# A recurrence of 3136 steps on one core: one chain of 32 images, or two chains of 16 in turn with longer filler matmuls

## The chip, the cores and the metric

The kernel runs on one core of a Trainium2 chip. The metric is the device time of one execution in microseconds (us), the median of several runs. The core has five engines: TensorE (PE; its weight loads are listed apart as PEld), VectorE (DVE), ScalarE (ACT), GpSimd (POOL) and SyncE (SP), which here issues all the DMAs. The profile tells of one more thing that matters here, the clock granted to TensorE: 1.00 in its rows is 2.4 GHz, and the lower level, 1.2 GHz, is half of that.

## What is computed

The program is two layers of a network on 32 images of 56 x 56 pixels with 128 channels. Layer 0 is windowed attention and a mixture of experts, layer 1 a focal convolution and, last, a recurrence over the 3136 pixels of each image. Only the recurrence is touched by the change. Cut to what matters:

```python
x = x + _L0_conv_ref(_ln_c(x), ...)          # attention in windows of 7 x 7
t = t + _L0_ffn_ref(_ln_t(t), ...)           # mixture of 8 experts
x = x + _L1_conv_ref(_ln_c(x), ...)          # focal convolution
t = t + _L1_ffn_ref(_ln_t(t), ...)           # the recurrence, below

def _L1_ffn_ref(x, W, V, gamma, beta):       # x: 32 images, 3136 tokens, 128 channels
    Wx = jnp.einsum('bti,hi->bth', x, W)
    mean, var = jnp.mean(flat, axis=0), jnp.var(flat, axis=0)      # flat: all tokens of Wx
    Wx = ((flat - mean) * jax.lax.rsqrt(var + BN_EPS) * gamma + beta).reshape(B, T, H)
    def step(yt, wx_t):
        yt = jax.nn.sigmoid(wx_t + yt @ V.T)
        return (yt, yt)
    _, ys = jax.lax.scan(step, y0, jnp.swapaxes(Wx, 0, 1))
    return jnp.swapaxes(ys, 0, 1)
```

Step t needs the result of step t - 1, so the 3136 steps are a chain. The 32 images are independent of one another.

## The kernel before

Six stages run one after the other; each has its own program on each engine, written out by hand, and semaphores between them. The stage that matters is `recurrent_stage`, the last one. The other five are the same before and after. Their names in the trace begin with `att`, `moe`, `foc`, `conv` and `mod`; those of the recurrence begin with `rec`.

The recurrent stage works in chunks of `TC` = 16 steps, 196 of them. The channels lie on the partitions, the images in the columns. For each chunk the tokens are loaded, normalized (DVE statistics, POOL scaling into `xn`), turned by TensorE into `pin` (four transposes, `turn_in`, L2407), copied by DVE into `xT`, and multiplied by the weights into the PSUM tile `ph` (`drive`, L2417: four pieces of 128 columns, each as four matmuls that write 32 partitions). After that `ph` holds wx_t for the 16 steps. Then each step of the chain is two links:

- TensorE adds V times the result of the step before onto 32 columns of `ph` (`add`, L2435: four fp32 matmuls, each with 32 columns of weights and 32 output partitions; the trace lists each as two records, so x8 for an add). It waits for the semaphore `moved`, and raises `added`.
- ScalarE takes the sigmoid of these 32 columns into `yT` (L2314). It waits for `added`, and raises `moved`.

The finished chunk is turned back by four transposes (`turn_out`, L2425, into `pout`), and DVE adds the residual (`finish`) and SP stores it. TensorE does the work of the neighbouring chunks between the adds: step 0 to 3 of a chunk hold one `turn_in` transpose each, steps 4 to 7 one `turn_out` each, steps 12 to 15 one piece of `drive` each. Behind the transposes, and in steps 8 to 11 alone, stands filler: four bf16 matmuls of 256 columns (384 in steps 8 to 11) into `p_idle` (L2466), whose result nobody reads. The order of TensorE's program is that of the Python text in `step`, and TensorE works through it in this order.

A matmul that takes 32 columns of weights fills a quarter of the array's columns; the trace writes it as 128*32 (rows * columns of the array). A transpose here is 128*128. Four matmuls of the form 128*32 that write different quarters of the partitions run beside one another. The words "tiling" and "form of the array" below mean this pair of numbers.

TensorE's loop is written out for two chunks (`U // 2`), and taken around some 97 times.

Of the kernel before, what the change touches and what calls it, by code (L numbers as in the profile page):

```python
# [19 lines left out]
ACT = mybir.ActivationFunctionType  # L20
AX = mybir.AxisListType

P = 128
C = 128
# [9 lines left out]
BANK = 512  # L34
# [60 lines left out]
def hold(eng, sem, value, ticks):  # L95


    eng.wait_ge(sem, value)
    eng.sem_inc(ticks, 1)
# [2067 lines left out]
def recurrent_stage(nc, B, x3, gram, W, w_t, v_t, gamma, beta, ident, out):  # L2167
# [6 lines left out]
    TC = 16  # L2174
    N = PIX // TC
    COLS_ = TC * B
    SUB = 4
    TT = TC // SUB
    ROWS = TT * B
# [3 lines left out]
    S = Stage(nc, "rec")  # L2183
    with S.ctx:
# [4 lines left out]
        vt = S.sb("vt", [C, C])  # L2189
# [4 lines left out]
        wbn = S.sb("wbn", [C, C])  # L2194
# [15 lines left out]
        idle_x = S.ctx.enter_context(nc.sbuf_tensor("rec_idle_x", [C, 384], mybir.dt.bfloat16))  # L2210
        p_idle = S.ps("p_idle", [P, BANK])

        pin = S.ps("pin", [P, BANK])
        pout = S.ps("pout", [P, BANK])
        ph = S.ps("ph", [P, 2, BANK])
        ps = S.ps("ps", [P, BANK])

        ticks = S.sem("ticks")
# [3 lines left out]
        stats_part, stats, eps_added, rstd_done, normed = (S.sem(k) for k in ("stats_part", "stats", "eps_added", "rstd_done", "normed"))  # L2222
        turned, xT_out = S.sem("turned"), S.sem("xT_out")
        driven = S.sem("driven")
        added, moved = S.sem("added"), S.sem("moved")
        y_turned, res_made = S.sem("y_turned"), S.sem("res_made")
        stored = S.sems("stored", 2)
        block = S.block()
        CONSTS = 16 * 7

        def column(t):

            at = (t % SUB) * ROWS + (t // SUB) * B
            return slice(at, at + B)

        @block.sync
        def _(sp):
# [65 lines left out]
        @block.scalar  # L2303
        def _(act):

            def step(n, first, last):
                a = n.slot(2)
                for t in range(TC):
                    cs = column(t)
                    if t == 0 and first >= 2:  # L2310
                        act.wait_ge(y_turned, n.val(1, -1))
                        act.sem_inc(ticks, 1)
                    act.wait_ge(added, n.val(TC, t + 1))
                    act.activation(yT[:, a, cs], ph[:, a, cs], ACT.Sigmoid).then_inc(moved, 1)  # L2314

            run_steps(act, N, U, step)

# [73 lines left out]
        def _(pe):  # L2391
# [19 lines left out]
            def drive(n, piece):  # L2411

                if piece == 0:
                    pe.wait_ge(xT_out, n.val(1, 1))
                cs = slice(piece * ROWS, (piece + 1) * ROWS)
                for r in range(0, C, 32):
                    ins = pe.matmul(ph[r:r + 32, n.slot(2), cs], wbn[:, r:r + 32], xT[:, n.slot(2), cs],  # L2417
                                    start=(piece == 0), stop=False, skip_group_check=True)
                if piece == SUB - 1:
                    ins.then_inc(driven, 1)  # L2420

# [6 lines left out]

            pe.wait_ge(setup, 13)

            def add(n, cs, before):


                for r in range(0, C, 32):
                    ins = pe.matmul(ph[r:r + 32, n.slot(2), cs], vt[:, r:r + 32], before, start=False, stop=True,  # L2435
                                    skip_group_check=True)
                ins.then_inc(added, 1)

            def step(n, first, last):
                a = n.slot(2)  # L2440
                if first == 0:
                    for sub in range(SUB):
                        turn_in(n, sub)
                    for piece in range(SUB):
                        drive(n, piece)
                for t in range(TC):
                    cs = column(t)
                    if t == 0 and first == 0:

                        add(n, cs, y0[:])  # L2450
                    else:
                        before = yT[:, a, column(t - 1)] if t else yT[:, 1 - a, column(TC - 1)]
                        pe.wait_ge(moved, n.val(TC, t))
                        add(n, cs, before)

                    if t < SUB and last < -1:
                        turn_in(n + 1, t)
                    if SUB <= t < 2 * SUB and first >= 1:
                        turn_out(n - 1, t - SUB, first - 1)
                    if t >= 3 * SUB:  # L2460
                        if last < -1:
                            drive(n + 1, t - 3 * SUB)
                        continue

                    for r in range(0, C, 32):
                        pe.matmul(p_idle[r:r + 32, 0:384 if t >= 2 * SUB else 256], idle_w[:, r:r + 32],  # L2466
                                  idle_x[:, 0:384 if t >= 2 * SUB else 256], start=True, stop=True)
                if last == -1:
                    pe.wait_ge(moved, n.val(TC, TC))
# [100 lines left out]
```

## Time and profile before

| what | value |
|---|---|
| median of 3 runs | 8683.52 us (8679.89 to 8687.49) |
| profiled execution, from its first to its last instruction | 8678.4 us |
| recurrent stage in it, from the first add to the last sigmoid | some 1838 us, from 6833 to 8671 us |
| TensorE busy over the span | 90% |
| granted clock in the middle of the recurrent stage | 1.00 |

The profile is of one execution. Its span is 5.1 us below the median of the runs, which is what lies around the span and between executions. Busy TensorE time is no measure here, since the modelled ends of matmuls overlap and since filler counts as work. How to read it: a step of the chain is found in the list of instructions in order of time, as the distance from one add to the next, and what stands between them tells which engine the chain waits for.

### The profile page before, as it was taken

The numbers are of one execution on the slowest core, as the hardware profiler recorded it, in microseconds if no ns is written. First come the engines' busy times: TensorE is split into PE (matmuls) and PEld (weight loads), VectorE is DVE, ScalarE is ACT, GpSimd is POOL, SyncE is SP. The second block draws the span as 40 slices with busy tenths as digits, with TensorE's granted clock in tenths as the row PEclk, the third lists the DMA queues.
The fourth block names the chain that finished last, engine by engine and source line by source line (L and its number), as shares of the span: only waits on it lengthen the run. The fifth ranks groups of instructions, "written<-read, shape, count | busy, mean of one in ns | idle before, by whom it ended". The sixth has DMA issues, their size and how long they took to land. (4 is left out here: it accounts for less than half of the span.)

```text
span 8678.4 us, 336810 instructions
## 1 busy us (share of the span) xinstructions
PE 7853.7 (90%) x120363; PEld 5180.1 (60%) x120363; DVE 6360.4 (73%) x21127; ACT 4495.5 (52%) x12517; POOL 5624.9 (65%) x6959
## 2 busy tenths in 40 slices
PE   7999999979999999869989999997999788888888
PEld 6777777754444444447767766655777555555554
DVE  7999999979999999878857777777888422222222
ACT  5666666645655555559933333335666333333333
POOL 8888888868888888768812222225777544444444
PEclk9999999989999999989999999999999899999999
DMA  1222222211111111148855555538888222222221
GB/s 52 58 58 58 58 58 58 57 55 58 57 56 56 56 59 57 63 157 300 295 189 187 180 188 190 193 132 219 232 231 229 77 56 57 56 56 56 56 57 53
DMA packets 797829, 958.44 MB, mean 110 GB/s; under 512 B 323100, under 2 KB 661825, under 8 KB 773584
## 3 DMA queue, kind: packets, MB, share of 16 engines
q1 hardware_dynamic: 797264, 952.06, 35.9%
q8 instruction: 214, 3.51, 0.2%
q14 instruction: 351, 2.88, 0.1%
HBM read 574.81 MB, written 453.35 MB: 118 GB/s over the span
## 5 line engine op out<-in xcount | busy, mean ns | idle before, releaser
L991 PE MATMUL moe_pe_out<-moe_we,moe_xnT 128*128 128x512 f32 x3136 | 1482.0, 607 | 179.2 <-DVE moe_acc L885 172.3
L1595 PE MATMUL conv_pc<-conv_c,conv_toep 64*64 64x432 f32 (+1 forms) x12260 | 1356.3, 527 | 2.5 <-ACT conv_c L1497 2.5
L2314 ACT ACTIVATE rec_yT<-rec_ph 128x32 f32<-128x32 f32 x3136 | 618.3, 197 | 1242.5 <-PE rec_ph L2435 1242.5
L787 ACT ACTIVATE moe_scaled<-moe_pe_out,moe_gate 128x128 f32<-128x128 f32 x3136 | 892.0, 367 | 692.6 <-PE moe_pe_out L991 690.6
L991 PEld LDWEIGHTS moe_pe_out<-moe_we,moe_xnT 128*128 128x128 f32 x3136 | 546.8, 191 | 942.4 <-issue 940.9
L1452 POOL TENSOR_TENSOR conv_g<-conv_c,conv_gate 128x896 f32<-128x896 f32 x128 | 366.6, 2864 | 1123.8 <-DVE conv_out L1565 1086.2
L2361 DVE COPY rec_xT<-rec_pin 128x512 f32<-128x512 f32 x196 | 135.6, 692 | 1240.1 <-PE rec_pin L2407 1240.1
L1595 PEld LDWEIGHTS conv_pc<-conv_c,conv_toep 64*64 64x64 f32 (+1 forms) x12260 | 855.3, 133 | 310.9 <-issue 108.8
L2435 PE MATMUL rec_ph<-rec_yT,rec_vt 128*32 128x32 f32 x25080 | 844.5, 207 | 195.5 <-ACT rec_yT L2314 120.8
L307 POOL TENSOR_SCALAR att_xn<-att_xin,att_mv,att_rstd 128x128 f32<-128x128 f32 x1024 | 881.9, 871 | 54.1 <-POOL att_rstd L303 54.1
L2435 PEld LDWEIGHTS rec_ph<-rec_yT,rec_vt 128*32 128x32 f32 x25080 | 496.9, 108 | 646.9 <-ACT rec_yT L2314 608.9
L2466 PE MATMUL rec_p_idle<-rec_idle_x,rec_idle_w 128*32 128x256 bf16 (+1 forms) x9408 | 718.5, 299 | 0.0
L725 POOL TENSOR_TENSOR moe_paired<-moe_scaled 128x256 f32<-128x256 f32 x784 | 582.6, 743 | 171.2 <-ACT moe_scaled L787 150.6
L2289 POOL TENSOR_SCALAR rec_xn<-rec_xin,rec_mv,rec_rstd 128x127 f32<-128x127 f32 x784 | 634.0, 821 | 41.5 <-POOL rec_rstd L2286 41.5
L2284 POOL TENSOR_SCALAR rec_rstd<-rec_mv 128x4 f32<-128x4 f32 x196 | 45.6, 233 | 893.0 <-DVE rec_mv L2356 863.7
L1595 PE MATMUL conv_pc<-conv_cin,conv_toep 64*64 64x448 f32 (+1 forms) x3048 | 522.1, 536 | 56.6 <-DMA conv_toep<-rows_dram 33.9
L1470 ACT ACTIVATE conv_c<-conv_pc,conv_gap 128x448 f32<-128x448 f32 x256 | 148.2, 630 | 689.7 <-PE conv_pc L1595 689.7
L718 POOL TENSOR_SCALAR moe_xn<-moe_xin,moe_mv,moe_rstd 128x127 f32<-128x127 f32 x560 | 483.8, 864 | 0.4 <-POOL moe_rstd L712 0.4
L1932 ACT ACTIVATE mod_z<-mod_xin,mod_nmean,mod_rstd_x 112x128 f32<-112x128 f32 x896 | 368.9, 483 | 168.8 <-DVE mod_nmean L2038 167.2
L330 ACT ACTIVATE att_prT<-att_pb 128x512 f32<-128x512 f32 x512 | 287.6, 597 | 234.1 <-PE att_pb L519 234.1
L312 POOL TENSOR_TENSOR att_xin<-att_xin,att_bproj 128x512 f32<-128x512 f32 x256 | 389.0, 1520 | 21.4
L733 POOL TENSOR_TENSOR moe_others<-moe_paired 128x128 f32<-128x128 f32 x784 | 360.4, 460 | 51.4 <-DVE moe_acc L930 33.9
(212 smaller groups left out, 19859.0 us busy)
## 6 DMA issues: line engine op xcount, KB each, us to landing
conv_toep<-rows_dram SPq DMA_DIRECT2D x32, 2304.0 KB, 13.7
c<-foc_cs SPq DMA_DIRECT2D x32, 1792.0 KB, 10.9
conv_cin<-c SPq DMA_DIRECT2D x32, 1792.0 KB, 10.2
ctx_all<-conv_out SPq DMA_DIRECT2D x32, 1792.0 KB, 6.5
att_xin<-x_windows SPq DMA_DIRECT2D x512, 98.0 KB
moe_xin<-x SPq DMA_DIRECT2D x112, 448.0 KB, 3.5
x<-moe_acc SPq DMA_DIRECT2D x112, 448.0 KB, 2.7
foc_xin<-x SPq DMA_DIRECT2D x32, 1568.0 KB, 8.3
```

The lines of the kernel that those rows point to most:

```text
L307: ins = pool.tensor_scalar(xn[:, a, t, :], xin[:, s, t, :], mv[:, a, t, 0:1], rstd[:, a, t:t + 1], ALU.subtract, ALU.mult)
L312: pool.tensor_tensor(xin[:, s, :, :], xin[:, s, :, :], bproj[:].unsqueeze(1).to_broadcast([P, PAIRS, C]), ALU.add).then_inc(bproj_added, 1)
L718: pool.tensor_scalar(xn[:, a, t, 0:C - 1], xin[:, n.slot(4), t, 0:C - 1], mv[:, a, t, 0:1], rstd[:, a, t:t + 1], ALU.subtract, ALU.mult).t ...
L725: pool.tensor_tensor(paired[:, b, :, :], scaled[:, b, 0:2, :], scaled[:, b, 2:4, :], ALU.add)\
L787: ins = act.activation(scaled[:, b, e, :], pe_out[:, b, 1, e * C:(e + 1) * C], ACT.Identity, scale=g)
L991: pe.matmul(pe_out[:, b, half, :], xnT[:, n.slot(2), t, :], we[:, half * 4:half * 4 + 4, :].rearrange("d e c -> d (e c)"), start=True, sto ...
L1595: return pe.matmul(image_pairs(pc[k], half)[m0:m1, :, i0:i1], w, tile[r0:r1, images(half), i0 + away:i1 + away], start=start, stop=True, s ...
L1932: ins = act.activation(z[:, b, t, 0:C], xin[:, m.slot(2), GRP * c + t, :], ACT.Identity, bias=nmean[:, b, t:t + 1], scale=rstd_x[:, b, t:t ...
L2289: ins = pool.tensor_scalar(xn[:, a, t, 0:C - 1], xin[:, n.slot(4), t, 0:C - 1], mv[:, a, t, 0:1], rstd[:, a, t:t + 1], ALU.subtract, ALU.mult)
L2314: act.activation(yT[:, a, cs], ph[:, a, cs], ACT.Sigmoid).then_inc(moved, 1)
L2435: ins = pe.matmul(ph[r:r + 32, n.slot(2), cs], vt[:, r:r + 32], before, start=False, stop=True, skip_group_check=True)
L2466: pe.matmul(p_idle[r:r + 32, 0:384 if t >= 2 * SUB else 256], idle_w[:, r:r + 32], idle_x[:, 0:384 if t >= 2 * SUB else 256], start=True, ...
```

## The change

The 32 images are split into two halves of 16 (`HALF`). Each half has its own chain: its own columns of PSUM (`ph` gets one more dimension, so that each half has a bank of its own for each of the two chunks in flight), its own `added` and `moved` semaphores, its own sigmoid of 16 columns. In each step TensorE's program is now: add of half 0, something, add of half 1, filler of 512 columns. The something is the `turn_in` transpose in steps 0 to 3, the `turn_out` transpose in steps 4 to 7, filler of 256 columns in steps 8 to 11, and a piece of `drive` in steps 12 to 15. `drive` writes the two halves by matmuls of 64 columns each, twice as many as before. The filler is no longer four matmuls of 32 weight columns, but two of 64 (`idle`). The filler that stood behind the transposes is gone; the one of 512 columns stands in every step. The loop over two chunks now holds 416 matmuls of the source, where it held 272. Semaphores that were waited for once in a step are waited for once per half.

```diff
-        ph = S.ps("ph", [P, 2, BANK])
+        ph = S.ps("ph", [P, 2, 2, BANK])
...
-        added, moved = S.sem("added"), S.sem("moved")
+        added, moved = S.sems("added", 2), S.sems("moved", 2)
...
-                    act.wait_ge(added, n.val(TC, t + 1))
-                    act.activation(yT[:, a, cs], ph[:, a, cs], ACT.Sigmoid).then_inc(moved, 1)
+                    for half in range(2):
+                        act.wait_ge(added[half], n.val(TC, t + 1))
+                        act.activation(yT[:, a, column(t, half)], ph[:, a, half, sums(t)], ACT.Sigmoid).then_inc(moved[half], 1)
...
-                for r in range(0, C, 32):
-                    ins = pe.matmul(ph[r:r + 32, n.slot(2), cs], wbn[:, r:r + 32], xT[:, n.slot(2), cs],
-                                    start=(piece == 0), stop=False, skip_group_check=True)
+                out = slice(piece * TT * HALF, (piece + 1) * TT * HALF)
+                for half in range(2):
+                    x = xT[:, n.slot(2), cs].rearrange("p (t b) -> p t b", b=B)[:, :, half * HALF:(half + 1) * HALF]
+                    for r in range(0, C, 32):
+                        ins = pe.matmul(ph[r:r + 32, n.slot(2), half, out].rearrange("p (t b) -> p t b", b=HALF), wbn[:, r:r + 32], x,
+                                        start=(piece == 0), stop=False, skip_group_check=True)
...
+            def add(n, t, half, first):
+                if t == 0 and first == 0:
+                    before = y0[:, 0:HALF]
+                else:
+                    before = yT[:, n.slot(2), column(t - 1, half)] if t else yT[:, 1 - n.slot(2), column(TC - 1, half)]
+                    pe.wait_ge(moved[half], n.val(TC, t))
                 for r in range(0, C, 32):
+                    ins = pe.matmul(ph[r:r + 32, n.slot(2), half, sums(t)], vt[:, r:r + 32], before, start=False, stop=True,
                                     skip_group_check=True)
-                ins.then_inc(added, 1)
+                ins.then_inc(added[half], 1)
+
+            def idle(columns):
+                for r in range(0, C, 64):
+                    pe.matmul(p_idle[r:r + 64, 0:columns], idle_w[:, r:r + 64], idle_x[:, 0:columns], start=True, stop=True)
...
                 for t in range(TC):
+                    add(n, t, 0, first)
                     if t < SUB and last < -1:
                         turn_in(n + 1, t)
-                    if SUB <= t < 2 * SUB and first >= 1:
+                    elif SUB <= t < 2 * SUB and first >= 1:
                         turn_out(n - 1, t - SUB, first - 1)
-                    if t >= 3 * SUB:
-                        if last < -1:
-                            drive(n + 1, t - 3 * SUB)
-                        continue
-
-                    for r in range(0, C, 32):
-                        pe.matmul(p_idle[r:r + 32, 0:384 if t >= 2 * SUB else 256], idle_w[:, r:r + 32],
-                                  idle_x[:, 0:384 if t >= 2 * SUB else 256], start=True, stop=True)
+                    elif t >= 3 * SUB and last < -1:
+                        drive(n + 1, t - 3 * SUB)
+                    else:
+                        idle(256)
+                    add(n, t, 1, first)
+                    idle(512)
```

How the instructions stand in TensorE's program before, inside the loop, at step 7 of a chunk (a `turn_out`) and steps 8 and 9 (filler alone). The last number of a row is partitions x columns of the output; a REGISTER_ALU works out the value of the next wait:

```order
L2435 MATMUL rec_ph<-rec_yT,rec_vt 32x32 x4
L2425 MATMUL rec_pout<-rec_idn,rec_yT 128x128
L2466 MATMUL rec_p_idle<-rec_idle_x,rec_idle_w 32x256 x4
L2453 REGISTER_ALU
L2435 MATMUL rec_ph<-rec_yT,rec_vt 32x32 x4
L2466 MATMUL rec_p_idle<-rec_idle_x,rec_idle_w 32x384 x4
L2453 REGISTER_ALU
L2435 MATMUL rec_ph<-rec_yT,rec_vt 32x32 x4
L2466 MATMUL rec_p_idle<-rec_idle_x,rec_idle_w 32x384 x4
```

The same place of TensorE's program now:

```order
L2450 MATMUL rec_ph<-rec_yT,rec_vt 32x16 x4
L2435 MATMUL rec_pout<-rec_idn,rec_yT 128x128
L2450 MATMUL rec_ph<-rec_yT,rec_vt 32x16 x4
L2456 MATMUL rec_p_idle<-rec_idle_x,rec_idle_w 64x512 x2
L2448 REGISTER_ALU
L2450 MATMUL rec_ph<-rec_yT,rec_vt 32x16 x4
L2456 MATMUL rec_p_idle<-rec_idle_x,rec_idle_w 64x256 x2
L2450 MATMUL rec_ph<-rec_yT,rec_vt 32x16 x4
L2456 MATMUL rec_p_idle<-rec_idle_x,rec_idle_w 64x512 x2
```

Between two adds of one chain stand now the other chain's add and one filler of 512 columns in two pieces of 64 partitions, beside the transpose or the shorter filler. Four changes of the form of the array lie in each step (32 to 128 or 64, back to 32, to 64, back to 32), where step 7 had two and steps 8 and 9 none.

Steps 12 and 13 in TensorE's program before, with the pieces of `drive`:

```order
L2435 MATMUL rec_ph<-rec_yT,rec_vt 32x32 x4
L2417 MATMUL rec_ph<-rec_xT,rec_wbn 32x128 x4
L2453 REGISTER_ALU
L2435 MATMUL rec_ph<-rec_yT,rec_vt 32x32 x4
L2417 MATMUL rec_ph<-rec_xT,rec_wbn 32x128 x4
```

And now:

```order
L2450 MATMUL rec_ph<-rec_yT,rec_vt 32x16 x4
L2427 MATMUL rec_ph<-rec_xT,rec_wbn 32x64 x8
L2450 MATMUL rec_ph<-rec_yT,rec_vt 32x16 x4
L2456 MATMUL rec_p_idle<-rec_idle_x,rec_idle_w 64x512 x2
L2448 REGISTER_ALU
L2450 MATMUL rec_ph<-rec_yT,rec_vt 32x16 x4
L2427 MATMUL rec_ph<-rec_xT,rec_wbn 32x64 x8
L2450 MATMUL rec_ph<-rec_yT,rec_vt 32x16 x4
L2456 MATMUL rec_p_idle<-rec_idle_x,rec_idle_w 64x512 x2
```

The `drive` steps had no filler, and every matmul in them had the form 128*32. Now the filler of 512 columns stands in them too, with two changes of form in each.

## Rows read from the trace of the kernel before

**Rows 1.** Stretches of the recurrent stage, middle part; columns in the first line.
```profile
core 0: us, PE busy (x) PEld busy (x) DVE busy (x) ACT busy (x) POOL busy (x), PEclk, DMA share, GB/s
7450.00:8050.00 600.00, 535.99 (x13860) 306.48 (x13856) 162.85 (x640) 202.27 (x1026) 289.04 (x387) 1.00 0.21 56
```

**Rows 2.** Who waited for whom from 6850 to 8650 us: total, times, longest.
```profile
ACT rec_yT L2314 <- PE rec_ph L2435: 1193.8, 3078, 0.8
```

**Rows 3.** Order of time, a filler step: start, duration (us), engine, instruction, [idle before].
```profile
7607.31 0.20 ACT L2314 ACTIVATE rec_yT<-rec_ph 128x32 f32<-128x32 f32 x1 [0.39 <-PE rec_ph L2435]
...
7607.56 0.27 PE L2435 MATMUL rec_ph<-rec_yT,rec_vt 128*32 128x32 f32 x8 [0.15 <-ACT rec_yT L2314]
...
7607.65 0.35 PE L2466 MATMUL rec_p_idle<-rec_idle_x,rec_idle_w 128*32 128x384 bf16 x4
...
7607.90 0.20 ACT L2314 ACTIVATE rec_yT<-rec_ph 128x32 f32<-128x32 f32 x1 [0.39 <-PE rec_ph L2435]
7608.15 0.16 PEld L2435 LDWEIGHTS rec_ph<-rec_yT,rec_vt 128*32 128x32 f32 x8 [0.41 <-ACT rec_yT L2314]
```

**Rows 4.** The same view, a step with a `turn_in` transpose.
```profile
7602.31 0.27 PE L2435 MATMUL rec_ph<-rec_yT,rec_vt 128*32 128x32 f32 x8
...
7602.51 0.33 PE L2407 MATMUL rec_pin<-rec_idn,rec_xn 128*128 128x128 f32 x1
...
7602.76 0.29 PE L2466 MATMUL rec_p_idle<-rec_idle_x,rec_idle_w 128*32 128x256 bf16 x4
...
7602.89 0.27 PE L2435 MATMUL rec_ph<-rec_yT,rec_vt 128*32 128x32 f32 x8
```

**Rows 5.** The same view, TensorE alone, a step with a piece of `drive`.
```profile
7600.55 0.27 PE L2435 MATMUL rec_ph<-rec_yT,rec_vt 128*32 128x32 f32 x8
7600.64 0.40 PE L2417 MATMUL rec_ph<-rec_xT,rec_wbn 128*32 128x128 f32 x8
```

**Rows 6.** The same view, TensorE alone, in the attention stage, two places.
```profile
600.94 0.60 PE L474 MATMUL att_pf<-att_idn,att_xn 128*128 128x128 f32 x4
...
903.22 0.82 PE L483 MATMUL att_pf<-att_xnT,att_wqkv 128*128 128x392 f32 x2
903.97 0.90 PE L532 MATMUL att_pb<-att_prT,att_vv 49*32 49x49 f32 x64
904.79 0.49 PE L491 MATMUL att_pf<-att_wqkv,att_xnT 128*49 128x64 f32 x10
```

**Rows 7.** Groups by form: busy us, mean ns of one | idle before.
```profile
L2435 PE MATMUL rec_ph<-rec_yT,rec_vt 128*32 128x32 f32 x25080 | 844.5, 207 | 195.5 <-ACT rec_yT L2314 120.8
L2466 PE MATMUL rec_p_idle<-rec_idle_x,rec_idle_w 128*32 128x256 bf16 x6272 | 461.1, 284 | 0.0
L2417 PE MATMUL rec_ph<-rec_xT,rec_wbn 128*32 128x128 f32 x6272 | 318.1, 275 | 0.8 <-DVE rec_xT L2361 0.8
L2466 PE MATMUL rec_p_idle<-rec_idle_x,rec_idle_w 128*32 128x384 bf16 x3136 | 273.5, 329 | 0.0
L1595 PEld LDWEIGHTS conv_pc<-conv_c,conv_toep 64*64 64x64 f32 x12248 | 853.1, 133 | 308.4 <-issue 106.4
L2435 PEld LDWEIGHTS rec_ph<-rec_yT,rec_vt 128*32 128x32 f32 x25080 | 496.9, 108 | 646.9 <-ACT rec_yT L2314 608.9
L330 ACT ACTIVATE att_prT<-att_pb 128x512 f32<-128x512 f32 x512 | 287.6, 597 | 234.1 <-PE att_pb L519 234.1
L2314 ACT ACTIVATE rec_yT<-rec_ph 128x32 f32<-128x32 f32 x3136 | 618.3, 197 | 1242.5 <-PE rec_ph L2435 1242.5
```

**Rows 8.** Code: two loops' stretches, then the DMA queues in the second.
```profile
432.92:460.75 27.83, 26.73 (x737) 21.21 (x738) 26.70 (x61) 17.43 (x33) 24.86 (x28) 1.00 0.20 54
...
4831.00:4921.00 90.00, 88.65 (x1017) 63.88 (x1013) 65.16 (x57) 34.35 (x64) 22.64 (x8) 1.00 0.55 187
...
q8 instruction: 9, 0.15, 0.8%
```

More of the change, by code:

```diff
@@ L2209, in recurrent_stage @@
         idle_w = S.ctx.enter_context(nc.sbuf_tensor("rec_idle_w", [C, C], mybir.dt.bfloat16))
-        idle_x = S.ctx.enter_context(nc.sbuf_tensor("rec_idle_x", [C, 384], mybir.dt.bfloat16))
+        idle_x = S.ctx.enter_context(nc.sbuf_tensor("rec_idle_x", [C, 512], mybir.dt.bfloat16))
         p_idle = S.ps("p_idle", [P, BANK])
@@ L2229, in recurrent_stage, with column, sums @@
         CONSTS = 16 * 7
-        def column(t):
-            at = (t % SUB) * ROWS + (t // SUB) * B
-            return slice(at, at + B)
+        HALF = B // 2
+        def column(t, half):
+            at = (t % SUB) * ROWS + (t // SUB) * B + half * HALF
+            return slice(at, at + HALF)
+        def sums(t):
+            at = (t % SUB) * TT * HALF + (t // SUB) * HALF
+            return slice(at, at + HALF)
         @block.sync
@@ L2308, in step @@
                 for t in range(TC):
-                    cs = column(t)
                     if t == 0 and first >= 2:
@@ L2429, in _ @@
             pe.wait_ge(setup, 13)
-            def add(n, cs, before):
+            def add(n, t, half, first):
[4 more added lines that the diff above has]
+                    pe.wait_ge(moved[half], n.val(TC, t))
                 for r in range(0, C, 32):
-                    ins = pe.matmul(ph[r:r + 32, n.slot(2), cs], vt[:, r:r + 32], before, start=False, stop=True,
+                    ins = pe.matmul(ph[r:r + 32, n.slot(2), half, sums(t)], vt[:, r:r + 32], before, start=False, stop=True,
                                     skip_group_check=True)
-                ins.then_inc(added, 1)
+                ins.then_inc(added[half], 1)
+            def idle(columns):
+                for r in range(0, C, 64):
+                    pe.matmul(p_idle[r:r + 64, 0:columns], idle_w[:, r:r + 64], idle_x[:, 0:columns], start=True, stop=True)
             def step(n, first, last):
-                a = n.slot(2)
                 if first == 0:
@@ L2446, in step @@
                 for t in range(TC):
[L2447 to L2454, printed above, removed]
+                    add(n, t, 0, first)
                     if t < SUB and last < -1:
                         turn_in(n + 1, t)
-                    if SUB <= t < 2 * SUB and first >= 1:
+                    elif SUB <= t < 2 * SUB and first >= 1:
                         turn_out(n - 1, t - SUB, first - 1)
-                    if t >= 3 * SUB:
-                        if last < -1:
-                            drive(n + 1, t - 3 * SUB)
-                        continue
-                    for r in range(0, C, 32):
-                        pe.matmul(p_idle[r:r + 32, 0:384 if t >= 2 * SUB else 256], idle_w[:, r:r + 32],
-                                  idle_x[:, 0:384 if t >= 2 * SUB else 256], start=True, stop=True)
+                    elif t >= 3 * SUB and last < -1:
[4 more added lines that the diff above has]
+                    idle(512)
                 if last == -1:
-                    pe.wait_ge(moved, n.val(TC, TC))
+                    for half in range(2):
+                        hold(pe, moved[half], n.val(TC, TC), ticks)
                     for sub in range(SUB):
```

## The prediction

> **What bounds the kernel now.** First the stretches of the recurrent stage [rows 1]: in 600 us there are 1026 sigmoids, one in 0.585 us; the clock is 1.00 throughout, the level of 2.4 GHz; every engine but TensorE is busy for less than half of the time. Since the stage takes 3136 steps, it takes 3136 x 0.585 = 1834 us, a fifth of the span, and every nanosecond of a step is worth 3.1 us.
>
> Then who waits for whom [rows 2]: ScalarE waited 1193.8 us for the adds in 3078 steps, 0.39 us a step; with its own 0.197 us [rows 7] this is the whole step. So the period is the round trip of one chain. The step with filler alone shows its links [rows 3]: the add begins at 7607.56, its sigmoid at 7607.90 (0.34 later), takes 0.20, and the next add begins 0.05 after its end. The add has waited: TensorE was done with the filler. In a step with a transpose there is no such wait [rows 4], yet the step is just as long, 7602.31 to 7602.89. There TensorE's own work fills the step by itself: add 0.20, transpose 0.25, filler 0.13. The reader is to see that TensorE has slack only where no transpose stands.
>
> The third thing is what a change of the array's form costs. The modelled end of a matmul is start plus duration. Where the next matmul has the same form, it begins 0.16 to 0.18 before that end: filler 7602.76 + 0.29 = 7603.05, the add at 7602.89 [rows 4]; add 7607.56 + 0.27 = 7607.83, filler at 7607.65 [rows 3]. Where the form changes, it begins only 0.07 to 0.08 before it: add (128\*32) to transpose (128\*128) 7602.58 against 7602.51, transpose to filler 7602.84 against 7602.76 [rows 4]; and with no transpose in it, 128\*128 to 49\*32 at 904.04 against 903.97, and 49\*32 to 128\*49 at 904.87 against 904.79 [rows 6]. So TensorE runs nearly empty at each change, and an add that takes 0.09 when filler of its own form follows [rows 3] takes 0.20 ahead of another form.
>
> **The change part by part.** TensorE takes its program in order, so in each step it does add, something, add, filler of 512, whichever chain is ready. I cost each piece as the time from its start to the start of the next.
>
> *Two chains.* Each chain has 16 columns. An fp32 column costs (275 - 207) / (128 - 32) = 0.7 ns [rows 7], so an add becomes 0.011 shorter, no more: the four weight loads and two records of each stay. A sigmoid shrinks by 16 x (597 - 197) / (512 - 32) = 0.013 [rows 7]. A chain's round trip becomes 0.585 - 0.024 = 0.561. That is the floor of a step, provided that TensorE's pieces sum to less; the two sigmoids, 2 x 0.184, fit into it.
>
> *Add ahead of another form:* 0.20 - 0.011, taken as 0.186 with the rounding of the rows (bounds 0.18 and 0.19). Of the same form, ahead of `drive`: 0.09 - 0.01 = 0.08.
>
> *Transposes*, unchanged: 0.256 (0.25 to 0.26) [rows 4].
>
> *Filler, two matmuls of 128\*64.* No row shows this form. The nearest is the filler of 128\*32 behind a transpose: 0.29 - 0.075 = 0.215 to a change of form [rows 4]. Weights of 64 columns take longer to load than of 32, by 133 - 108 = 25 ns in fp32 [rows 7]; here between 0 and that, and I take 0.007, since bf16 is half the bytes and part is hidden. So 0.222 for 256 columns (0.215 to 0.24). For 512 there are 256 columns more, at (329 - 284) / 128 = 0.35 ns [rows 7] 0.09, at the full 2.4 GHz 0.107: I take 0.325 (0.31 to 0.34). The two halves of the array work side by side, as the four quarters do in [rows 3].
>
> *`drive` pieces.* The same columns in twice the matmuls. Add to `drive` is 0.09 and `drive` 0.40 long, 0.17 of which overlaps the next add of the same form [rows 5]: 0.32, less 0.01 for the shorter add, 0.315 for both (0.30 to 0.33).
>
> *The form changes* decide. The rows show a change from 32 to 128, 128 to 32, and between two partial forms (49\*32 to 128\*49), all with the same result. 32 to 64 columns at 128 rows stands in no row. The Trainium skill states it in general, in TensorEngine Tiling (Array Packing), Key Properties: "Changing tiling mode (not just tile) drains the TensorE". By that rule the pair here is no exception; by the rows alone it is a close neighbour of what they show, and I cost it so and price the opposite below.
>
> *Sums.* Steps with a transpose (8 of 16): 0.186 + 0.256 + 0.186 + 0.325 = 0.953. Steps with both fillers (4): 0.186 + 0.222 + 0.186 + 0.325 = 0.919. Steps with `drive` (4): 0.315 + 0.186 + 0.325 = 0.826. The mean is (8 x 0.953 + 4 x 0.919 + 4 x 0.826) / 16 = 0.913. All three lie far above the 0.561 of a chain, so TensorE's order becomes the bound, and the latency that the second chain hides is not on the path any more. Against 0.585 that is +0.328 a step, 3136 x 0.328 = +1029 us. The span goes from 8678.4 to 9707; with the 5.1 us between span and median, 9712. I say **9710**.
>
> *At nothing:* DVE, POOL and SP have 16 x 0.9 = 14.6 us for a chunk instead of 9.4, and waited before. The second sigmoid lies beside the filler. The waits per half stand in TensorE's queue ahead of the other chain's add, but the sigmoid waited for was over some 0.35 us earlier. The first and last dozen steps run at the lower clock and may add some 10 us, within the range. If the filler were not there (its cover for nothing but the clock), the sum would be 0.6 to 0.63 in the transposing steps and the chain 0.561 elsewhere: even then not much is won.
>
> **The bounds.** All low ends together: steps of 0.92, 0.885 and 0.79, mean 0.879, +922 us, 9605. All high ends: 0.98, 0.955 and 0.86, mean 0.944, +1126 us, 9810. I widen the lower side to 9560, since the form of 64 is not shown and the next add's weights may come in a little sooner.
>
> **The rivals.**
> *The array goes from 32 to 64 columns without running empty.* For it: no row shows this pair, and the weights of 32 and 64 columns might share a setting. Against: every change that the rows do show costs the same, 49\*32 to 128\*49 included. Then an add ahead of filler takes 0.08, filler 0.225 (512) or 0.13 (256): steps of 0.186 + 0.256 + 0.08 + 0.225 = 0.747, 0.561 (the chain; TensorE's pieces sum to 0.515) and 0.315 + 0.08 + 0.225 = 0.62, mean 0.669, +262 us, **8946**. With the drain in one direction only, the mean is about 0.78 to 0.79 and the time some **9300**.
> *The chains win.* If no change of form at all cost more than columns, the longest step would be 0.08 + 0.15 (four transposes in a row end after 0.60 in all [rows 6]) + 0.08 + 0.225 = 0.535, below 0.561; the stage would run at the chain's 0.561, 0.024 x 3136 = 75 us faster, **8608**. The place is TensorE's order in the transposing steps, and the point from which it decides is a sum under 0.561. Against it speak both changes in [rows 4], which alone make 0.44 of add and transpose.
> *Code loading.* The loop now has 256 x 4 (adds) + 64 x 4 (`drive`) + 16 x 2 (transposes) + 80 x 2 (filler) = 1472 matmul and weight-load records where it had 864. The attention loop has 737 + 738 = 1475 in an iteration of 27.83 us, and no block of code is read in it; the convolution's has 1017 + 1013 in 90 us, and 9 blocks are read [rows 8]. So 1472 should stay loaded. The Trainium skill, in Runtime: NRT & Kernel Launch, Instruction fetch mechanics, gives TensorE room for 2048 instructions, but also says that a branch back beyond two pages of code must wait for a read; by the first the loop stays, by the second each turn stalls. The rows of the attention loop agree with the first. If it stalled, one read in each of 97 turns: 0.8% of 16 engines' 90 us over 9 blocks is 1.28 us each [rows 8], 124 us on top, **9836**.
> *The two halves of the filler run one after the other:* +0.21 in every step and more in four, over **10,400**. [rows 3] show four quarters at once, so this is remote.
>
> **How the numbers follow.** Forecast 0.84; 32 to 64 for free 0.05, one way 0.03; code loading 0.03; halves in turn 0.01; chains win 0.03; and 0.01 that terms cancel to about the time before. Of the forecast's 0.84 nearly all lies in 9560 to 9830, so this range holds the time about 8 times in 10 and need not reach a rival. A measurement of this kernel can tell about 0.2%, 17 us, from no change. Faster by more 0.03, within it 0.01, slower 0.96.
>
> **What would show it.** Right: ScalarE's 6272 sigmoids of about 184 ns, two in each 0.91 us; no idle time of TensorE before an add; filler of 512 beginning 0.07 before the modelled end of the add ahead of it, and an add 0.07 before the filler's end; steps of three lengths, 0.95, 0.92 and 0.83. Wrong: filler beginning 0.08 after the start of an add (first rival); adds that still wait for sigmoids in most steps (chains win); reads of code in the middle of the stage (code loading).

## The result, and the profile after

The changed kernel takes 9737.3 us (9733.2 to 9737.8), the kernel before 8685.5 in the runs beside it: 1.121 times as long, 95% interval 1.1195 to 1.1223. The forecast was 9710, with a range from 9560 to 9830. The profiled execution of the changed kernel spans 9735.2 us, 1056.8 more than before. Some executions of several kernels here take some 40 us longer, and in the one of them that was traced (the run in two quarters, below) the attention stage, which the change does not touch, ended at 1876.0 us instead of 1832 to 1838, so differences are also read from the recurrent stage alone, from the start of its first sigmoid to that of its last: 1838.0 us before, 2891.7 us now.

The stretch in the middle of the recurrent stage, in the view of [rows 1]:

```profile
core 0: us, PE busy (x) PEld busy (x) DVE busy (x) ACT busy (x) POOL busy (x), PEclk, DMA share, GB/s
7450.00:8050.00 600.00, 600.00 (x15031) 361.15 (x15029) 104.07 (x410) 240.43 (x1306) 185.12 (x246) 1.00 0.14 36
```

There are 1306 sigmoids, each of half the images, so 653 steps in 600 us: 0.919 us a step where [rows 1] gave 0.585. The clock is 1.00 as before, so TensorE is not slower; it has more to do in each step. It is busy without a gap, 600.00 of 600. Who waited for whom from 6850 to 9700 us, to set against [rows 2] (total, times, longest):

```profile
ACT rec_yT L2321 <- PE rec_ph L2450: 1605.2, 5373, 0.6
PEld rec_ph L2450 <- issue: 705.4, 3098, 0.4
...
PEld rec_ph L2450 <- ACT rec_yT L2321: 0.2, 1, 0.2
```

ScalarE still waits for adds, but no add waits for a sigmoid any more, except one. TensorE's own order sets the step. In order of time (start, duration, engine, instruction), first a step with a transpose, then one with both fillers, then one with a piece of `drive`:

```profile
7994.47 0.26 PE L2450 MATMUL rec_ph<-rec_yT,rec_vt 128*32 128x16 f32 x8
7994.65 0.33 PE L2435 MATMUL rec_pout<-rec_idn,rec_yT 128*128 128x128 f32 x1
7994.91 0.26 PE L2450 MATMUL rec_ph<-rec_yT,rec_vt 128*32 128x16 f32 x8
7995.10 0.41 PE L2456 MATMUL rec_p_idle<-rec_idle_x,rec_idle_w 128*64 128x512 bf16 x2
7995.44 0.26 PE L2450 MATMUL rec_ph<-rec_yT,rec_vt 128*32 128x16 f32 x8
...
8000.21 0.26 PE L2450 MATMUL rec_ph<-rec_yT,rec_vt 128*32 128x16 f32 x8
8000.40 0.30 PE L2456 MATMUL rec_p_idle<-rec_idle_x,rec_idle_w 128*64 128x256 bf16 x2
8000.62 0.26 PE L2450 MATMUL rec_ph<-rec_yT,rec_vt 128*32 128x16 f32 x8
8000.81 0.41 PE L2456 MATMUL rec_p_idle<-rec_idle_x,rec_idle_w 128*64 128x512 bf16 x2
8001.15 0.26 PE L2450 MATMUL rec_ph<-rec_yT,rec_vt 128*32 128x16 f32 x8
...
7988.18 0.26 PE L2450 MATMUL rec_ph<-rec_yT,rec_vt 128*32 128x16 f32 x8
7988.26 0.41 PE L2427 MATMUL rec_ph<-rec_xT,rec_wbn 128*32 128x64 f32 x16
7988.49 0.23 PE L2450 MATMUL rec_ph<-rec_yT,rec_vt 128*32 128x16 f32 x8
7988.65 0.41 PE L2456 MATMUL rec_p_idle<-rec_idle_x,rec_idle_w 128*64 128x512 bf16 x2
7988.99 0.26 PE L2450 MATMUL rec_ph<-rec_yT,rec_vt 128*32 128x16 f32 x8
```

The steps are 0.97, 0.94 and 0.81 us long. At every change of form the next matmul begins 0.07 to 0.08 before the modelled end of the one ahead, here also between 32 and 64 columns: 8000.21 + 0.26 = 8000.47 against 8000.40, 8000.81 + 0.41 = 8001.22 against 8001.15. Where the form stays (add to `drive`, 7988.44 against 7988.26) it is 0.18. This is the pair that no row of before showed, and it behaves as the others.

### The profile page after: what moved, and what is told of

The parts are those of the page before. It is cut to its first block and busy times, and to the rows that moved or that the text cites. A ratio compares the mean times of both kernels' runs of the same rounds, so it can differ in the third digit from the quotient of the medians.

```text
span 9735.2 us, 399581 instructions
## 1 busy us (share of the span) xinstructions
PE 9107.2 (94%) x150179; PEld 6007.5 (62%) x150179; DVE 6362.9 (65%) x21127; ACT 5035.8 (52%) x15653; POOL 5631.5 (58%) x6959
## 5 line engine op out<-in xcount | busy, mean ns | idle before, releaser
L2321 ACT ACTIVATE rec_yT<-rec_ph 128x16 f32<-128x16 f32 x6272 | 1155.2, 184 | 1759.2 <-PE rec_ph L2450 1654.5
L2450 PEld LDWEIGHTS rec_ph<-rec_yT,rec_vt 128*32 128x32 f32 x50160 | 1010.3, 108 | 1001.3 <-issue 717.9
L2450 PE MATMUL rec_ph<-rec_yT,rec_vt 128*32 128x16 f32 x50160 | 1583.0, 192 | 0.0
L2456 PE MATMUL rec_p_idle<-rec_idle_x,rec_idle_w 128*64 128x512 bf16 (+1 forms) x7864 | 1518.3, 383 | 0.0
L1595 PEld LDWEIGHTS conv_pc<-conv_c,conv_toep 64*64 64x64 f32 (+1 forms) x12260 | 877.1, 133 | 282.0 <-issue 95.3
L2456 PEld LDWEIGHTS rec_p_idle<-rec_idle_x,rec_idle_w 128*64 128x64 bf16 x7864 | 430.9, 106 | 108.9
```

The lines of the kernel that those rows point to most:

```text
L1595: return pe.matmul(image_pairs(pc[k], half)[m0:m1, :, i0:i1], w, tile[r0:r1, images(half), i0 + away:i1 + away], start=start, stop=True, s ...
L2321: act.activation(yT[:, a, column(t, half)], ph[:, a, half, sums(t)], ACT.Sigmoid).then_inc(moved[half], 1)
L2450: ins = pe.matmul(ph[r:r + 32, n.slot(2), half, sums(t)], vt[:, r:r + 32], before, start=False, stop=True, skip_group_check=True)
L2456: pe.matmul(p_idle[r:r + 64, 0:columns], idle_w[:, r:r + 64], idle_x[:, 0:columns], start=True, stop=True)
```

## The experiments

Theory: the change of form between adds (32 columns) and filler (64) makes TensorE run empty twice more in each step, and with that its pieces sum to more than the round trip of a chain. Rivals: the columns of filler cost, in whatever form; the step is held by another link; code is loaded.

**Filler of the adds' form, in four quarters.**

```diff
-                for r in range(0, C, 64):
-                    pe.matmul(p_idle[r:r + 64, 0:columns], idle_w[:, r:r + 64], ...)
+                for r in range(0, C, 32):
+                    pe.matmul(p_idle[r:r + 32, 0:columns], idle_w[:, r:r + 32], ...)
```

> The changed kernel with its filler of 256 and 512 columns in four matmuls of 32 weight columns (the form of the adds) where it has two of 64; columns and places stay. Theory (a change of the array's form lets TensorE run empty, and this sets the step): the add ahead of the filler shrinks from 0.19 to 0.08 us and the filler from 0.33 to 0.22; steps of 0.75 us with a transpose, 0.56 (one chain's round trip) with both fillers, 0.59 with a piece of drive, mean 0.66; time 8,935 us. Rival (the columns of filler cost, whatever their form): steps and time stay, 9,737 us.

Measured 9613 us (9595 to 9630): the theory's time missed by far, and yet not for the rival's reason. Where no code was read, the steps were as short as the theory gives or shorter (0.56 to 0.58 with filler or `drive`, 0.72 with a transpose), but every second turn of TensorE's loop (32 steps) took some 34 us instead of 20.9. At such a turn, in order of time, TensorE alone:

```profile
8161.90 0.40 PE L2456 MATMUL rec_p_idle<-rec_idle_x,rec_idle_w 128*32 128x512 bf16 x4
8166.98 0.31 PE L2450 MATMUL rec_ph<-rec_yT,rec_vt 128*32 128x16 f32 x8 [4.68 <-issue]
8167.22 0.48 PE L2414 MATMUL rec_pin<-rec_idn,rec_xn 128*128 128x128 f32 x1
```

TensorE stands still for 4.68 us with no semaphore to wait for (in the kept trace it is the branch at the loop's end that takes 4.9 us on average at such turns, and 0.2 at the others), and the transpose after it takes 0.48 instead of 0.33: the clock has fallen (granted 0.84 on average from 7450 to 8050 us). The DMA queues from 7000 to 8600 us show why, ahead of those of the changed kernel from 7000 to 9600:

```profile
q8 instruction: 252, 4.13, 1.2%
...
q1 hardware_dynamic: 67889, 92.76, 13.6%
q14 instruction: 19, 0.16, 0.0%
```

252 blocks of code are read here through q8, nine in each of the long turns and none in the short ones, and none in the changed kernel. The queue q14, with a read now and then in both, goes with no standstill. The filler's four matmuls instead of two make 1632 records in the loop where the changed kernel has 1472, and it does not stay loaded. So this run mixed two causes, and the next two runs take them apart.

**Two quarters: the adds' form, the loop as long as in the changed kernel.**

```diff
-                for r in range(0, C, 64):
-                    pe.matmul(p_idle[r:r + 64, 0:columns], idle_w[:, r:r + 64], ...)
+                for r in range(0, 64, 32):
+                    pe.matmul(p_idle[r:r + 32, 0:columns], idle_w[:, r:r + 32], ...)
```

> The changed kernel with each filler as two matmuls of 32 weight columns, so that the filler has the adds' form and the loop as many matmuls as in the changed kernel (a quarter of the array's columns each, half of it unused). It repeats the run with four quarters without its longer code. Theory (change of form): transposing steps 0.72 us, all others 0.56, mean 0.64, no code read in the middle of the stage, 8,850 us. Rival (the columns cost, and the four quarters gained little because columns are what counts): above 9,600 us.

Measured 8891 us (8869 to 8913), no code read. A step with a transpose, in order of time, TensorE alone:

```profile
7908.60 0.26 PE L2450 MATMUL rec_ph<-rec_yT,rec_vt 128*32 128x16 f32 x8
7908.68 0.38 PE L2456 MATMUL rec_p_idle<-rec_idle_x,rec_idle_w 128*32 128x512 bf16 x2
7908.74 0.37 PE L2450 MATMUL rec_ph<-rec_yT,rec_vt 128*32 128x16 f32 x8
7909.05 0.33 PE L2435 MATMUL rec_pout<-rec_idn,rec_yT 128*128 128x128 f32 x1
7909.30 0.26 PE L2450 MATMUL rec_ph<-rec_yT,rec_vt 128*32 128x16 f32 x8
```

The filler begins 0.08 after the add (0.19 in the changed kernel). Of the next add's eight records, four begin 0.06 after the filler and four some 0.16 later, which fits the two quarters that the filler leaves free. The step is 0.70, the others 0.56 to 0.58. With columns, places and number of matmuls as in the changed kernel, 870 of the 1054 us by which the recurrent stage had grown are gone (it takes 2022.0 us; by the medians, 846 of 1052). The forecast was 8850. This filler covers only half of the array, so the free half could have had a part in the gain. But the run with four quarters covers all of it, and its undisturbed turns take 20.9 us against 20.5 here and 29.4 in the changed kernel. The form was the cost. What stays above the kernel before is the transposing steps, whose own two changes of form no filler touches, and some 0.3 us where the loop turns back.

**The same form, twice the matmuls of half the columns.**

```diff
+                for part in range(2):
+                    cs = slice(part * columns // 2, (part + 1) * columns // 2)
                     for r in range(0, C, 64):
-                        pe.matmul(p_idle[r:r + 64, 0:columns], ...)
+                        pe.matmul(p_idle[r:r + 64, cs], ...)
```

> The changed kernel with each filler cut into twice as many matmuls of half the columns, the form of 64 columns kept: the loop gets as many records as in the run with four quarters (1632 against 1472), and nothing else changes. Theory (the longer loop does not stay loaded): blocks of code are read throughout the stage and a turn waits for them, 9,950 to 10,400 us. Rival (what the run with four quarters lost was due to its filler or its clock, not to code): 9,740 us, no code read.

Measured 10,518 us, more than the upper end. The stretch from 7450 to 8050 us, and TensorE's code queue from 7000 to 8600:

```profile
7450.00:8050.00 600.00, 545.14 (x12895) 332.74 (x12893) 79.01 (x310) 185.85 (x1010) 140.87 (x188) 0.80 0.12 31
...
q8 instruction: 275, 4.51, 1.3%
```

The steps that are not disturbed keep their length (0.97, 0.94, 0.81), but there are 505 steps in 600 us instead of 653: code is read, and the clock is at 0.80 on average. So code loading is real, 160 records above the changed kernel. It costs some 780 us, where the prediction gave 124 for one read a turn. In 63 of 95 turns nine blocks are read, and such a turn takes 41.9 us instead of 29.5. Some 4.4 us of this is the standstill at the branch. The rest lies in the steps behind it: most of the next chunk's take 1.3 to 1.45 us at the lower clock.

**One chain, filler in halves.** In the kernel before only the filler's form is changed, as `C, 32` to `C, 64` and `r + 32` to `r + 64`.

> The kernel before (one chain of 32 images) with its filler of 256 and 384 columns in two matmuls of 64 weight columns where it has four of 32. Theory: the eight steps with a transpose become 0.20 + 0.26 + 0.22 = 0.68 us, since the filler is now drained before the next add; the steps with filler alone stay at 0.585, because add and filler take 0.47 there and the chain is waited for anyway; mean 0.63, time 8,833 us. Rival (the two halves are harmless, and only the doubled adds and the longer filler cost): 8,685 us. Second rival (the two halves run one after the other): transposing steps of 0.79 and filler steps of 0.63, 9,050 us.

Measured 8876 us (8855 to 8898, two runs), slower than the kernel before by 1.1 to 3.0%. The recurrent stage takes 2008.2 us, 170 more than before, where the theory gives 148. A step with a transpose, TensorE alone, then two steps with filler alone:

```profile
7905.42 0.27 PE L2435 MATMUL rec_ph<-rec_yT,rec_vt 128*32 128x32 f32 x8
7905.62 0.33 PE L2407 MATMUL rec_pin<-rec_idn,rec_xn 128*128 128x128 f32 x1
7905.88 0.30 PE L2466 MATMUL rec_p_idle<-rec_idle_x,rec_idle_w 128*64 128x256 bf16 x2
...
7900.51 0.27 PE L2435 MATMUL rec_ph<-rec_yT,rec_vt 128*32 128x32 f32 x8
7900.71 0.35 PE L2466 MATMUL rec_p_idle<-rec_idle_x,rec_idle_w 128*64 128x384 bf16 x2
7901.10 0.27 PE L2435 MATMUL rec_ph<-rec_yT,rec_vt 128*32 128x32 f32 x8
```

The transposing step grows from 0.585 to 0.69, the others stay at 0.585 although their filler now begins 0.20 after the add instead of 0.09 [rows 3]. A change of form costs nothing where the chain is waited for anyway, and its whole price where TensorE has no slack. The halves run side by side: a transposing step would be 0.79 if they did not.

**256 columns instead of 512 behind the second half.** One word: `idle(512)` becomes `idle(256)`.

> The changed kernel with 256 columns instead of 512 in the filler behind the second half, all else as it is. Theory (TensorE's order is the bound in every step): each step loses 256 columns at 2.4 GHz, 0.107 us; 3136 x 0.107 = 335 us, 9,402 us. Rival (another link, a chain's round trip or ScalarE, holds the step): less than 100 us, above 9,640 us.

Measured 9429 us (9413 to 9445); the recurrent stage takes 2566.7 us, 325 less than in the changed kernel, where 335 were forecast. The stretch from 7450 to 8050 us:

```profile
7450.00:8050.00 600.00, 600.00 (x17013) 408.50 (x17014) 117.12 (x460) 272.13 (x1477) 207.74 (x276) 1.00 0.15 41
```

1477 sigmoids are 738.5 steps, 0.812 us each, 0.106 less than in the changed kernel, nearly all of the forecast 0.107. So nothing but TensorE's order holds the step.

**Any change of form.** The filler becomes one matmul of 128 weight columns over the whole array:

```diff
-                for r in range(0, C, 64):
-                    pe.matmul(p_idle[r:r + 64, 0:columns], idle_w[:, r:r + 64], ...)
+                pe.matmul(p_idle[:, 0:columns], idle_w[:], idle_x[:, 0:columns], start=True, stop=True)
```

> The changed kernel with each filler as one matmul of 128 weight columns, same columns and places. Theory (any change of form makes TensorE run empty, whichever two forms they are): the same steps as in the changed kernel, give or take the longer load of the weights, 9,740 to 9,850 us. Rival (only the pair of 32 and 64 is dear): 9,400 us or less.

Measured 9680 us, 0.6% below the changed kernel, so the range was missed on the low side and the rival is out. A filler behind an add of the second half:

```profile
7908.12 0.39 PE L2455 MATMUL rec_p_idle<-rec_idle_x,rec_idle_w 128*128 128x512 bf16 x1
7908.44 0.25 PE L2450 MATMUL rec_ph<-rec_yT,rec_vt 128*32 128x16 f32 x8
```

Again the next matmul begins 0.07 before the end. The filler takes 0.32 where two halves take 0.34, though its weights are twice as wide. The loads of the filler's weights (least, median and longest time in ns, behind the colon), in the kernel before, the changed kernel and this run:

```profile
L2466 PEld LDWEIGHTS rec_p_idle<-rec_idle_x,rec_idle_w x9408: 91/93/133, 6833.9 to 8667.9; 128*32 128x32 bf16 x196
...
L2456 PEld LDWEIGHTS rec_p_idle<-rec_idle_x,rec_idle_w x7864: 106/106/128, 6836.6 to 9726.8; 128*64 128x64 bf16 x197
...
L2455 PEld LDWEIGHTS rec_p_idle<-rec_idle_x,rec_idle_w x3932: 95/95/103, 6840.0 to 9670.0; 128*128 128x128 bf16 x197
```

So 128 columns load in 95 ns where 64 take 106, which is some 0.011 of the 0.02. The Trainium skill says in TensorE: Matmul & The Clock Gate, Weight-path perf modes, that bf16 weights of full width load faster; the trace agrees, 95 ns against 106.

**No filler at all.** `idle(256)` and `idle(512)` are left out; `p_idle` stays unwritten.

> The changed kernel without any filler (p_idle is not written; no result depends on it). Theory: TensorE's pieces sum to 0.53 us in the transposing steps and less elsewhere, so each step is one chain's round trip, 0.561 us at a granted clock of 1.00: about 8,615 us, a little faster than the kernel before. If the clock falls to 1.2 GHz without filler: adds of 0.26, transposes of 0.31 and a chain of 0.63, mean step 0.65, about 8,890 us. Rival (two chains in turn have a cost of their own besides form and filler): well above both.

Measured 8733 us (8716 to 8772), between the two cases named, 0.4% slower than the kernel before:

```profile
7450.00:8050.00 600.00, 544.95 (x20424) 419.39 (x20428) 158.06 (x621) 297.13 (x1994) 282.05 (x375) 0.85 0.20 55
```

Steps at the full clock are 0.558 long, the round trip of a chain of 16 images that the prediction had at 0.561; but the granted clock is 0.85 on average, and 997 steps in 600 us are 0.602 each. With the new order of VectorE (below) and still no filler:

> The run without filler, with VectorE's statistics of chunk n + 2 ahead of the copy of chunk n + 1. Theory (at the chunk's end the first transpose waits for the normalized chunk, and this loop of TensorE, VectorE and POOL holds the chunk at 9.6 us): that wait goes, the boundary steps fall from 0.8 to 1.2 us to 0.56 to 0.65, and the time to 8,640 to 8,690 us; the clock stays below 1.00 in places. Rival (the clock alone makes those steps long): 8,730 us as without the new order.

Measured 8721 us (8698 to 8778), not the 8640 to 8690 of the theory. The medians are not clearly apart, but the recurrent stage is 34 us shorter in the traces (1855.5 us against 1889.6): three transposes wait for normalizing instead of 40, and the granted clock is 0.91 instead of 0.85 in the middle. Why the clock is higher is not shown. The steps where the loop turns back are as long as before (0.92 to 1.19 us). I had put them down to normalizing; that was wrong, as the next run shows.

**Two chains where they fit.** Filler of the adds' form only where TensorE has room, and VectorE's statistics earlier:

```diff
                 for t in range(TC):
                     add(n, t, 0, first)
...
+                    elif 2 * SUB <= t < 3 * SUB:
+                        idle(384, 4)
                     add(n, t, 1, first)
-                    idle(512)
+                    if 2 * SUB <= t < 3 * SUB:
+                        idle(384, 4)
+                    elif t >= 3 * SUB:
+                        idle(256, 2)
...
-                if last < -1:
-                    drive(n + 1)
                 if last < -2:
                     ...
                     layer_stats(n + 2)
+                if last < -1:
+                    drive(n + 1)
```

Here `idle(columns, parts)` writes `parts` quarters, each with 32 weight columns.

> Two chains with filler of the adds' form alone, and only where TensorE has room: 384 columns in four quarters behind each half in steps 8 to 11, 256 in two quarters behind the second half in steps 12 to 15, none beside the transposes; 1472 records in the loop as in the changed kernel. Besides, VectorE takes the statistics of chunk n + 2 before the copy of chunk n + 1, so that normalizing does not wait for the transposes. Theory: TensorE's pieces stay below a chain's round trip of 0.559 us in all steps, and the statistics come early enough: 8,605 us, 0.9% faster than the kernel before, at a granted clock near 1.00. Rival (without filler beside the transposes the clock falls): 8,650 to 8,730 us.

Measured 8677 us, 0.998 of the kernel before (0.9965 to 0.9994): faster, but by far less than the forecast (9 us in the recurrent stage, 1828.7 us, where 83 were forecast). From the run before it differs by the filler alone, and the stage is 27 us shorter, so here the filler pays for itself. The clock is 1.00, and 29 of the loop's 32 steps take 0.56 to 0.57. Two places cost more, together some 60 us. Where the loop turns back, once in 32 steps, 0.41 us is lost (order of time, TensorE and ScalarE):

```profile
7715.29 0.28 PE L2456 MATMUL rec_p_idle<-rec_idle_x,rec_idle_w 128*32 128x256 bf16 x2
7715.53 0.18 ACT L2321 ACTIVATE rec_yT<-rec_ph 128x16 f32<-128x16 f32 x1 [0.15 <-PE rec_ph L2450]
7715.70 0.26 PEld L2450 LDWEIGHTS rec_ph<-rec_yT,rec_vt 128*32 128x32 f32 x8 [0.34 <-ACT rec_yT L2321]
```

The sigmoid that this add needs was over at 7715.38; the add should have begun at 7715.43 and began at 7715.70. The branch lies between: in the kept trace it takes from 7715.35 to 7715.56. The view puts the wait down to a sigmoid, but that is not it. The rest of the 0.41 lies mostly in the add itself, whose sigmoid begins 0.39 after it, instead of 0.32 elsewhere. And in step 8 of each chunk 0.11 us is lost, where the distance between the two chains changes from that of the transposing steps (0.45) to that of the filler steps; the next run bears this out, since it keeps the distance and the loss is gone.

**The pair first, then the work.** In the same kernel both adds stand at the head of the step and the work behind them: transposes in steps 0 to 7, `drive` and `idle(256, 2)` in 8 to 11, twice `idle(384, 4)` in 12 to 14, nothing in 15.

> The last candidate (two chains, filler of the adds' form, VectorE's statistics ahead of its copy) with another order in TensorE's step: both adds at once, and the work behind them; transposes in steps 0 to 7, drive and 256 columns of filler in two quarters in steps 8 to 11, 768 columns in four quarters in steps 12 to 14, nothing in step 15, where the loop turns back. Theory (that candidate loses 0.41 us where the loop turns back, once in 32 steps, since TensorE has only a short gap between adds there, and 0.11 us in step 8, where the distance between the two chains has to change): both go, every step is a round trip of 0.559 us, 8,620 us, 0.8% faster than the kernel before. Rival (the two sigmoids stand so close that ScalarE delays the second chain, or the branch costs as before): 8,660 us or above.

Measured 8632 us, 0.9946 of the kernel before (0.993 to 0.9963), the fastest of all. The view of [rows 1], and two steps at 7909 us:

```profile
7450.00:8050.00 600.00, 583.43 (x24033) 407.11 (x24025) 167.76 (x669) 299.48 (x2136) 300.62 (x400) 1.00 0.22 59
...
7909.24 0.36 PE L2450 MATMUL rec_ph<-rec_yT,rec_vt 128*32 128x16 f32 x16
7909.56 0.28 ACT L2321 ACTIVATE rec_yT<-rec_ph 128x16 f32<-128x16 f32 x2 [0.27 <-PE rec_ph L2450]
7909.80 0.36 PE L2450 MATMUL rec_ph<-rec_yT,rec_vt 128*32 128x16 f32 x16
```

1068 steps in 600 us, 0.562 each; the recurrent stage takes 1781.6 us, 56 less than before. Where the loop turns back a step takes 0.57 to 0.74, on average 0.65, not 0.97. The two sigmoids lie side by side in 0.28 us.

**The same with VectorE's old order.** The last piece of the diff above is undone.

> The same kernel with VectorE's order as it was (copy first, then the statistics). Theory (the loop of transposes, copy, statistics and normalizing takes some 9.2 us, more than 16 steps of 0.559, 8.94 us): the first transpose of a chunk waits some 0.2 us, 16 to 40 us slower than with the new order. Rival (the loop fits into a chunk): the same time within 0.2%.

Measured 8655 us (0.9951 to 0.9977 of the kernel before), 23 us above the new order. What the transposes of `turn_in` waited for over the whole span, first here, then with the new order (total, times):

```profile
POOL rec_xn L2296: 44.9, 188
...
POOL rec_xn L2296: 8.5, 3
```

In 188 of 196 chunks the first transpose waits for the normalized chunk, 0.24 us a time. The step there takes 0.69 in one of the loop's two chunks, and 0.56 or 0.68 in the other, instead of 0.56. So this loop does not fit into 16 steps of 0.559, though it fits into 16 of 0.585. Not all of the difference is this wait: in eight turns of the loop the clock fell for a while and some 2 us were lost each time, with the new order in three, so some 10 of the 27 us by which the stage is longer (1809.1 us) belong to the clock.

## Why the prediction was right

**The bound before** was read rightly: a round trip of one chain. The run with one chain and filler in halves grew by 0.10 in the steps without slack and by nothing in the others (but for those at the loop's turn).

**The change of form** was the one step without a row of its own. It was costed by its neighbours, and the trace after bears it out: 0.07 before the end at each change between 32 and 64. The run in two quarters shows what that is worth: 870 us of the 1054 in the recurrent stage. The Trainium skill names the rule in general, in TensorEngine Tiling (Array Packing), Key Properties: "Changing tiling mode (not just tile) drains the TensorE". The trace agrees.

**The terms**, each from start to start, forecast and measured (medians of the trace after): add ahead of another form 0.186 and 0.185; transpose 0.256 and 0.258; filler of 256 0.222 and 0.230; of 512 0.325 and 0.336; add with `drive` 0.315 and 0.311; the add behind `drive`, ahead of the filler, 0.186 and 0.161. Steps 0.953, 0.919, 0.826 forecast, 0.966, 0.937, 0.808 measured, mean 0.913 and 0.919. The filler was taken too short in every step, in part for its weights: those of 64 columns load in 106 ns where those of 32 take 93, 0.013 us more, and 0.007 had been taken. The add behind `drive` was taken too long. These errors have opposite signs and cancel in part, so the mean is nearer than its parts, which is luck. Of the 28 us by which the span exceeds the forecast some 21 lie in the steps, some 4 in the first and last chunks, and 3 outside the stage, whose first sigmoid begins at 6835.3 instead of 6832.8 us. The some 10 us that the prediction allowed for steps at the lower clock can at most be those 4.

**What did not hold, with next to no effect on the sum.** The [rows 5] do not show that 0.17 of `drive` overlaps the next add: that add, at 7601.14, waited for its sigmoid and began 0.10 after the modelled end of `drive`. The 0.17 came from rows where the form stays, and the trace after bears it out (0.18). The 0.6 to 0.63 for transposing steps without filler does not follow from the prediction's terms, which give some 0.52, less than a chain's round trip; the run without filler has 0.558 there at the full clock. The high ends of a step with both fillers sum to 0.96, not 0.955, and 16 x 0.9 is 14.4.

**The rivals.** The free change from 32 to 64 is refuted by the trace after. That the chains win was not refuted as a mechanism: with the changes of form out of the way of the chain it came true, to 8632 instead of the 8608 of the sum. Code loading did not decide here, as said, but its margin was much narrower than I thought, and its price six times what I gave (780 us against 124): a turn with reads costs 12.3 us, not 1.28, since nine blocks are read in it, TensorE stands still, and its clock falls.

**What I did not see.** The prediction put the filler's cover at nothing but the clock, and that is what it is worth: without it the clock is at 0.85 on average, and the two chains win nothing. And the prediction priced nothing for the turn of the loop. The changed kernel hides it: 32 steps by themselves sum to what a turn takes, 29.4 us.

## What to carry to other kernels

Two independent chains hide latency only while all that the in-order engine does in a step fits below one chain's round trip; sum it from start to start, with each change of the array's form at its drained price. Keep one form in a tight loop, filler included, or put the changes where the engine waits anyway. When a candidate adds matmuls to a loop, look at the code queue first, since a loop that no longer stays loaded can cost more than what is being tried.

## What was not expected of the hardware

- A loop of 1472 matmul and weight-load records stays loaded, and one of 1632 does not: nine blocks are read in every second turn (four quarters) or two turns of three (twice the matmuls), with a standstill of some 4.7 us and a granted clock of 0.80 to 0.84 on average. The limit lies between, and where was not tried. The Trainium skill gives TensorE room for 2048 instructions (Runtime: NRT & Kernel Launch, Instruction fetch mechanics). In the traces the two loops hold some 1510 and 1670 instructions in all, register and branch instructions included, so a loop well within that room is read again here; what else takes up room is open. The same section says that a branch back beyond two pages of code must wait for a read; in the loop of 1472 records no branch did.
- A loop's turn costs TensorE about 0.4 us when the next add comes soon after the last one, and nothing when the chain leaves a gap (0.585 us in the kernel before, at the turn as elsewhere). The branch itself takes 0.21 to 0.24 us in all the traces, where no code is read at it.
- Sigmoids of 184 ns that stand close to each other overlap: two take 0.28 us.
